# Merging the entry of the attention into its tile loop, with the exponentials made head by head on ScalarE

## The reference

```
x = x + graph_network(layernorm(x))                  # ends in batch norm and relu
h = layernorm(x)
weights = softmax(((h @ W_x + b_x) @ W_slice + b_slice) / temp)   # over the 64 slices of a head
norm    = weights.sum(over the nodes)
token   = einsum("bhnc,bhng->bhgc", h @ W_fx + b_fx, weights) / (norm + 1e-5)
...                                                  # attention among the 64 tokens of a head
x = x + (weights applied to the tokens) @ W_out + b_out
x = x + hypergraph_network(layernorm(x)); x = x + experts(layernorm(x))
```

## Time and profile before

| what | value |
|---|---|
| time, median of 3 runs | 2929.48 us (2929.36 to 2931.73) |
| the profiled execution, its time | 2930.67 us |
| its span in the profile | 2928.9 us |
| TensorE busy | 2408.9 us (82%) |
| VectorE busy | 1091.7 us (37%) |
| ScalarE busy | 388.4 us (13%) |
| GpSimd busy | 879.8 us (30%) |
| entry of the attention | about 1548 to 1575 us of the span |
| attention loop | about 1575 to 1710 us |

### The profile page before, as it was taken

How to read it: one execution, slowest core, us unless ns; L and a number is a source line. 1 busy time by engine, 2 the same in 40 slices (tenths; PEclk the granted TensorE clock), 3 DMA queues, 4 the chain that set the end, 5 groups by cost and what they waited for, 6 DMA issues and landing times.

```text
span 2928.9 us, 40346 instructions
## 1 busy us (share of the span) xinstructions
PE 2408.9 (82%) x14486; PEld 1801.0 (61%) x14486; DVE 1091.7 (37%) x2853; ACT 388.4 (13%) x839; POOL 879.8 (30%) x627
## 2 busy tenths in 40 slices
PE   5285556832759999999996879999999995999997
PEld 2151113521547776777773347888888884888886
DVE  7688885502321011111116855112220577111111
ACT  0030000000015000005002212000110002222221
POOL 6888887788830000000002410000000000233332
PEclk6595557976979999999997979999999997999999
DMA  9922226926460999990351000444344434567766
GB/s 340 293 1 0 0 1 216 287 2 168 75 179 0 233 249 266 186 204 0 101 191 51 0 0 1 129 146 131 123 140 151 149 126 136 169 202 213 209 188 176
DMA packets 297780, 397.71 MB, mean 136 GB/s; under 512 B 177973, under 2 KB 241228, under 8 KB 297610
## 3 DMA queue, kind: packets, MB, share of 16 engines
q1 hardware_dynamic: 115530, 268.24, 28.9%
q10 hardware_dynamic: 109760, 108.20, 14.0%
q0 software_dynamic: 72400, 20.04, 8.2%
HBM read 279.30 MB, written 99.82 MB: 129 GB/s over the span
## 4 chain that ended last, share of the span: by engine, by line
PE 60%; POOL 15%; DVE 8%; issue 7%; DMA 6%; ACT 1%; ACTq 1%; DVEq 1%; POOLq 0%; SPq 0%
PE ps L1919 14%; PE ps L2218 8%; PE ps L2219 8%; POOL at_counts L595 7%; POOL odd_counts L595 7%; PE ps L2312 7%; PE ps L2303 7%; PE ps L1846 4%; DMA odd_counts<-tarena 3%; PE ps L1937 3%; PE ps L2050 2%; PE ps L2151 2%; PE ps L2174 2%; DMA at_counts<-harena 2%; DVE late L1127 1%
## 5 line engine op out<-in xcount | busy, mean ns | idle before, releaser
L2218 PE MATMUL ps<-harena,ring 128*128 128x257 f16 (+1 forms) x2500 | 551.5, 272 | 8.0 <-DVE harena L1513 3.6
L2219 PE MATMUL ps<-harena,ring 128*128 128x256 f16 x2500 | 551.3, 271 | 0.0
L1919 PE MATMUL ps<-ring,harena 128*128 128x320 f16 x3800 | 511.8, 297 | 1.4 <-ACT tarena L758 0.8
L1919 PEld LDWEIGHTS ps<-ring,harena 128*128 128x128 f16 x3800 | 371.6, 98 | 138.1 <-issue 3.1
L595 POOL DMA_INDIRECT at_counts<-harena x208 | 332.5, 1599 | 89.7 <-issue 79.0
L595 POOL DMA_INDIRECT odd_counts<-harena x208 | 328.1, 1578 | 72.4 <-issue 60.9
L1127 DVE SCALAR_TENSOR_TENSOR late<-ps,ring 128x512 f16<-128x512 f32 x416 | 287.3, 746 | 21.5 <-issue 18.4
L1808 PE MATMUL ps<-harena,ident 104*128 104x512 f32 x208 | 187.4, 1018 | 117.7 <-DVE late L1127 116.7
L2218 PEld LDWEIGHTS ps<-harena,ring 128*128 128x128 f16 x2500 | 243.2, 97 | 44.2 <-DVE harena L1551 5.6
L2219 PEld LDWEIGHTS ps<-harena,ring 128*128 128x128 f16 x2500 | 241.7, 97 | 31.1
L1937 PE MATMUL ps<-feat,wl 128*128 128x320 f32 x448 | 126.2, 443 | 112.9 <-DVE feat L1209 111.8
(11 more groups left out here) (394 smaller groups left out, 2444.9 us busy)
## 6 DMA issues: line engine op xcount, KB each, us to landing
ring<-at_counts SPq DMA_DIRECT2D x145, 800.0 KB
ring<-L_ffn_W SPq DMA_DIRECT2D x64, 1024.0 KB, 5.1
ring<-ad_counts SPq DMA_DIRECT2D x50, 800.0 KB
at_counts<-tarena ACTq DMA_DIRECT2D x5, 4000.0 KB
odd_counts<-tarena ACTq DMA_DIRECT2D x5, 4000.0 KB
at_counts<-ring ACTq DMA_DIRECT2D x25, 800.0 KB
ad_counts<-xrows ACTq DMA_DIRECT2D x25, 800.0 KB, 8.0
xrows<-odd_counts SPq DMA_DIRECT2D x20, 800.0 KB
```

The source lines that it names most:

```text
L1919: ins = M(ps[:, 2 * f + h, 0:c], part[:, t, (2 * k + f) * P:(2 * k + f + 1) * P], chunk[q][:, s, h * HB:h * HB + c], start=(t == 0 and par ...
L2218: M(ps[:, i, 0:wide], lhs, hh[:, t, 0:wide], start=(t == 0), stop=False)
L2219: ins = M(ps[:, i, 0:F], lhs, hl[:, t, :], start=False, stop=(t == T - 1))
```

## The change

The entry is no stage of its own any more.

- ScalarE rectifies in place, `tfeat` to `tfeat`, all five blocks in one go.
- TensorE turns the first ENTRY_AHEAD = 7 tiles in front of the loop (`entry_turn`), into banks 0 to 3, and tile t+7 in the turn of tile t, into bank 6. The bias of the logits is spread before that, into bank 7.
- VectorE adds seven tiles and takes their statistics ahead of the loop, and the others in it, one a turn, at the turn's end. The variances, the root and the reciprocal are now made block by block (`entry_variance`, `entry_sqrt`, `entry_scale`, at the places that `stats_block` names: behind turns 2, 7, 12 and 17 for blocks 1 to 4).
- The loop is written out in full on all four engines, and the order in a turn is another: VectorE normalizes tile t+1, then does the shift of tile t-1, then the softmax of tile t-2; TensorE makes the tokens of tile t-3.
- VectorE no longer subtracts the maximum and no longer sums the heads: it negates the 8 maxima. ScalarE makes the exponentials in eight activations of 64 columns, with the negated maximum as bias and the head's sum as accumulator output.

```diff
+        ENTRY_AHEAD = 7
+        def stats_block(t):
+            b, k = divmod(t + ENTRY_AHEAD + 1, BT)
+            return b - 1 if k == 0 and 1 <= b - 1 < NB else None
+        def entry_bank(t):
+            return t % 4 if t < ENTRY_AHEAD else 6
...
 ScalarE
-            with act.Fori(0, NB) as b:
-                wait(tps, b * BT + 1)
+            for b in range(NB):
                 for f in range(2):
-                    nc.scalar.activation(feat[:, f, :], tfeat[:, f, nodes(b)], ACT.Relu,
+                    nc.scalar.activation(tfeat[:, f, nodes(b)], tfeat[:, f, nodes(b)], ACT.Relu,
...
-            ln_sqrt(5)
+            def entry_sqrt(b):
+                wait(ln_var, 5 + b)
+                tiles = slice(b * BT, b * BT + BT)
+                nc.scalar.activation(ln_s[:, tiles], ln_r[:, tiles], ACT.Sqrt).then_inc(ln_std, 1)
+            entry_sqrt(0)
...
-            def f_exps(t, i):
+            def f_exps(t):
                 wait(f_sub, t + 2)
-                nc.scalar.activation(logit[:, i % 3, :], logit[:, i % 3, :], ACT.Exp).then_inc(f_exp, 1)
+                for h in range(HEADS):
+                    columns = logit[:, t % 3, h * G:(h + 1) * G]
+                    ins = nc.scalar.activation(columns, columns, ACT.Exp, bias=hmax[:, t % 3, h:h + 1],
+                                               accum_out=hsum[:, t % 3, h:h + 1])
+                ins.then_inc(f_exp, 1)
...
-            three_stages(act.Fori(1, NB), f_copy, f_exps, f_weights)
+            for t in range(T + 3):
+                if t < T:
+                    f_copy(t, t % BT)
+                if t >= 1 and stats_block(t - 1) is not None:
+                    entry_sqrt(stats_block(t - 1))
+                if 1 <= t <= T:
+                    f_exps(t - 1)
+                if t >= 3:
+                    f_weights(t - 3)
...
 VectorE
-            dve.wait_ge(ent[3][1], T + 1)
-            layernorm_stats(5)
+            def add_gnn(t):
+                dve.wait_ge(tps, t + 2)
+                V.tensor_tensor(xrows[:, t, :], ps[:, entry_bank(t), 0:F], xrows[:, t, :], ALU.add).then_inc(lo, 1)
+                dve.wait_ge(lo, t + 2)
+                o.mark(V.bn_stats(ln_st[:, t, :], xrows[:, t, :]))
+            def entry_variance(b):
+                o.settle()
+                norm_variance(slice(b * BT, b * BT + BT))
+            def entry_scale(b):
+                tiles = slice(b * BT, b * BT + BT)
+                dve.wait_ge(ln_std, 5 + b)
+                step(V.reciprocal(ln_r[:, tiles], ln_s[:, tiles]))
...
-                V.tensor_tensor(logit[:, s, :].rearrange(H8, h=HEADS), logit[:, s, :].rearrange(H8, h=HEADS),
-                                hmax[:, s, :].unsqueeze(2).to_broadcast([P, HEADS, G]), ALU.subtract).then_inc(f_sub, 1)
+                V.tensor_scalar(hmax[:, s, :], hmax[:, s, :], -1.0, None, ALU.mult).then_inc(f_sub, 1)
...
-                step(V.tensor_reduce(hsum[:, s, :], logit[:, s, :].rearrange(H8, h=HEADS), AX.X, ALU.add))
                 step(V.reciprocal(hrec[:, s, :], hsum[:, s, :]))
-                if not isinstance(t, int) or t >= 2:
-                    dve.wait_ge(f_sum, t)
-                dve.wait_ge(f_used, t + (BT - 1))
+                if t >= 3:
+                    dve.wait_ge(f_sum, t - 1)
+                    dve.wait_ge(f_used, t + BT - 2)
...
-            three_stages(o.loop_from(1, NB, 4 * BT), f_normal, f_shift, f_softmax, third_early=True)
+            for t in range(ENTRY_AHEAD):
+                add_gnn(t)
+                if t == BT - 1:
+                    entry_variance(0)
+            entry_scale(0)
+            f_normal(0, 0)
+            for t in range(T + 2):
+                if t + 1 < T:
+                    f_normal(t + 1, (t + 1) % BT)
+                if 1 <= t <= T:
+                    f_shift(t - 1)
+                if t >= 2:
+                    f_softmax(t - 2)
+                if t + ENTRY_AHEAD < T:
+                    add_gnn(t + ENTRY_AHEAD)
+                if stats_block(t) is not None:
+                    entry_variance(stats_block(t))
+                if t >= 1 and stats_block(t - 1) is not None:
+                    entry_scale(stats_block(t - 1))
...
 TensorE
+            pe.wait_ge(x_in, 48)
+            M(ps[:, 7, :], ones[0:1, :], slice_bias[:, :], start=True, stop=True).then_inc(f_lg, 1)
+            def entry_turn(t):
+                pe.wait_ge(rows, t // BT * 2 + 2)
+                if t >= ENTRY_AHEAD:
+                    pe.wait_ge(lo, t + 1)
+                elif t >= 4:
+                    pe.wait_ge(lo, t - 2)
+                for f in range(2):
+                    ins = nc.tensor.transpose(ps[:, entry_bank(t), f * P:(f + 1) * P], tfeat[:, f, t * P:(t + 1) * P], ident[:, :])
+                ins.then_inc(tps, 1)
+            for t in range(ENTRY_AHEAD):
+                entry_turn(t)
...
-            three_stages(pe.Fori(1, NB), f_turn, f_logits, f_tokens)
+            for t in range(T + 3):
+                if t < T:
+                    f_turn(t, t % BT)
+                if t + ENTRY_AHEAD < T:
+                    entry_turn(t + ENTRY_AHEAD)
+                if 1 <= t <= T:
+                    f_logits(t - 1, (t - 1) % BT)
+                if t >= 3:
+                    f_tokens(t - 3, (t - 3) % BT)
```

More of the change, by code:

```diff
@@ L645, in _ @@
             pool.wait_ge(late_w, 16 * 17)
-            with pool.Fori(0, NB) as b:
-                for i in range(BT):
-                    r = bass.ds(b * BT + i, 1)
-                    pool.wait_ge(f_rows, b * BT + (i + 1))
-                    pool.nop(nofuse=True)
-                    nc.gpsimd.tensor_tensor(xrows[:, r, :], xrows[:, r, :], bout.unsqueeze(1), ALU.add).then_inc(f_bias, 1)
-                    pool.wait_ge(f_sw, b * BT + (i + 1))
-                    pool.wait_ge(f_sum, b * BT + (i + 1))
-                    pool.nop(nofuse=True)
-                    nc.gpsimd.tensor_tensor(weight_sum, weight_sum, sweight[:, i % 3, :], ALU.add).then_inc(f_sum, 1)
+            for t in range(T):
+                pool.wait_ge(f_rows, t + 1)
+                nc.gpsimd.tensor_tensor(xrows[:, t, :], xrows[:, t, :], bout, ALU.add).then_inc(f_bias, 1)
+                pool.wait_ge(f_sw, t + 1)
+                pool.wait_ge(f_sum, t + 1)
+                nc.gpsimd.tensor_tensor(weight_sum, weight_sum, sweight[:, t % 3, :], ALU.add).then_inc(f_sum, 1)
             pool.wait_ge(c_x, NB)
@@ L885, in block_sqrt @@
             def block_sqrt(b):
-                wait(ln_var, 6 + b)
+                wait(ln_var, 5 + NB + b)
                 tiles = slice(b * BT, b * BT + BT)
@@ L939, in route_sqrt @@
                 blk = bass.ds(b * BT, BT)
-                wait(ln_var, b * 2 + (NB + 6 + k))
+                wait(ln_var, b * 2 + (2 * NB + 5 + k))
                 nc.scalar.activation(ln_s[:, blk], ln_r[:, blk], ACT.Sqrt).then_inc(ln_std, 1)
@@ L2062, in _ @@
             pe.wait_ge(agg[2][0], NB * 2 + 2)
-            with pe.Fori(0, NB) as b:
-                pe.wait_ge(rows, b * 2 + 2)
-                for i in range(BT):
-                    pe.wait_ge(lo, b * BT + (2 if i == 4 else 1))
-                    for f in range(2):
-                        ins = nc.tensor.transpose(ps[:, i % 4, f * P:(f + 1) * P], feat[:, f, i * P:(i + 1) * P], ident[:, :])
-                    ins.then_inc(tps, 1)
+            pe.wait_ge(x_in, 48)
[11 more added lines that the diff above has]
+                entry_turn(t)
             pe.sem_inc(f_used, BT)
@@ L2088, in f_logits @@
                 pe.wait_ge(f_tcp, t + 2)
-                pe.wait_ge(f_sub, t + (2 - before(i)))
+                pe.wait_ge(f_sub, max(t, 1))
                 for d in range(2):
-                    ins = M(ps[:, i % 2, :], feat[:, d, i * P:(i + 1) * P], wxs[:, d, :], start=(d == 0), stop=(d == 1))
+                    ins = M(ps[:, t % 2, :], feat[:, d, i * P:(i + 1) * P], wxs[:, d, :], start=(d == 0), stop=(d == 1))
                 ins.then_inc(f_lg, 1)
```

41 lines of the change are left out of this document (14 added, 27 removed).

## The result

The changed kernel takes 2912.22 us (median of 4 runs, 2910.68 to 2918.32) against 2929.42 before: ratio 0.9933, 95% interval 0.9903 to 0.9962. Five more runs gave 2915.05 (2910.21 to 2919.93), ratio 0.9952 (0.994 to 0.9965). It is faster by 0.5 to 0.7%, and the forecast of 2914.4 lies between the two medians. The sum behind the forecast was less good than that, as the two traces show when only the changed stage is measured.

What follows compares the result with a forecast made beforehand. It took a relay entry with little overlap, then a loop with VectorE and TensorE near their end, as the bound. Entry -17.5, fill +0.5, loop +0.9, drain +1.0 made -15.1 us: 2914.4 us, range 2903 to 2922.

Steps and rivals of the forecast that it cites:

- Entry, -17.5 us: Ahead of the loop: in-place rectification and only seven tiles up front bring the first normalization 17.5 us earlier.
- The knot, 5.22 us: Loop with entering tiles: bank 6 waits for VectorE's addition, logits queue behind its transposes, next shift waits; 5.22 us a turn.
- 16 of them: Loop: the number of turns with tiles still entering, each put at 5.22 us; 8 turns without entering tiles follow.
- Stats turns, +1.5: Four loop turns with a block's variance: seven tiny VectorE instructions beside GpSimd cost 0.3 to 0.5 us each, 1.5 in all.
- Cold start, +2.9: First loop turns: TensorE at the half clock for one and a half turns, each 1.9 us dearer, +2.9 us.
- Turns without entering tiles, 4.35: Last 8 loop turns: TensorE's own work sets 4.35 us a turn, the middle of 4.2 and 4.47.
- Drain, +1.0: Behind the last shift: longer uncovered exponentials and one more token step, less subtraction and sums, +1.0 us.
- Exponentials, 2.7 us a tile: ScalarE in the loop: eight 64-column activations with accumulator take 2.7 us a tile (2.0 to 3.6), hidden except at the drain.
- The first (the knot does not bind): Loop rival, chance 0.12: all turns take 4.35 us, 13.9 us less, 2900.5 us in whole.
- The second (clock): Loop rival, chance 0.07: TensorE's clock stays low; all 16 turns at half clock give +36 us, near 2965.
- The third: Stats turns rival, chance 0.12: a table switch holds ScalarE twice its load, 2.6 us more each; +5.6 us, 2920.0.
- The fourth rival: Loop rival, chance 0.05: ScalarE becomes the bound, deciding from 0.53 us a head; at 0.6 the kernel takes 2943 us.

Runs made afterwards that it cites:

- a_swap: The changed kernel with TensorE issuing a tile's logits ahead of the entry transposes of tile t+7; 2894.86 us, ratio 0.9892 to the kernel before.
- a_early: The changed kernel with VectorE's addition and statistics of tile t+7 moved ahead of the softmax of tile t-2; 2899.82 us, ratio 0.9902 to the kernel before.
- a_wide: The changed kernel with the old softmax: one 512-column exponential, subtraction and head sums on VectorE; 2938.19 us, ratio 1.0039 to the kernel before.
- a_busy: The changed kernel with eight unneeded one-column ScalarE operations behind each tile's exponentials; 2911.22 us, ratio 0.9927 to the kernel before.
- a_noroot: The changed kernel with a copy in place of the block variances' square root, so no table switches in the loop; 2908.18 us, ratio 0.992 to before.
- b_heads: The kernel before with only the exponentials head by head, without VectorE's subtraction and head sums; 2944.72 us, ratio 1.0049 to the kernel before.

## Why the prediction was right, and where its sum was off

The direction, the place of the gain and the thing that paces the loop came out as written. By its steps:

- **Entry, -17.5 us**: -17.8.
- **Fill, +0.5**: 6.30 against 5.83, +0.5.
- **The knot, 5.22 us**: 5.16 in most turns, with both waits predicted (0.65 for "0.6", 1.15 for "about 1.3"). a_swap and a_early each open it, a_wide lengthens it by what it adds.
- **"16 of them"** is right for the knot, but 8 turns without entering tiles was one too many. From shift 16 to 17 VectorE still adds tile 24 and does its block's statistics, without a transposed tile behind it on TensorE, and that took 5.48 us: 17 turns with VectorE's addition and 7 without, +0.9. The 17 were 0.7 cheaper in all than 5.22 and 4.32 for the first.
- **Stats turns, +1.5**: 0.3 each, 1.2. They are what VectorE's work takes beyond the knot, not a part of the knot.
- **Cold start, +2.9: off by 1.6.** One turn ran at a mean clock of 0.75 and cost 1.3; in two other runs of kernels with the same start the clock was 1.00 and it cost nothing. I had taken one and a half turns at the half clock.
- **Turns without entering tiles, 4.35**: 4.08 on the mean, -1.9 over seven, the largest miss in the loop. Even the lower of my two bounds, 4.2 by starts, was too high.
- Together the loop was 118.2 us, not 121.8: -2.8 in place of +0.9.
- **Drain, +1.0**: from tile 24's shift to its tokens it is 5.48 us against 4.59, the +0.9 that I meant. But the stage's end came 0.4 earlier, not 1.0 later, since the last token matmuls and transposes ran faster: the granted clock from their start to the stage's end was 1.00, and 0.64 before. After (timeline):

```profile
1694.68 0.20 DVE L1423 RECIPROCAL harena<-harena 128x8 f32<-128x8 f32 x1 [1.94 <-ACT harena L882]
...
1695.72 1.98 PE L2143 MATMUL ps<-harena,feat 128*128 128x512 f32 x4 [0.50 <-DVE harena L1427]
1697.55 0.60 PE L2145 MATMUL ps<-ident,harena 128*128 128x128 f32 x4
```

  Before, the last two of these rows:

```profile
1706.68 2.83 PE L2098 MATMUL ps<-harena,feat 128*128 128x512 f32 x4 [2.03 <-DVE harena L1405]
1709.31 1.06 PE L2101 MATMUL ps<-ident,harena 128*128 128x128 f32 x4
```

  TensorE stood idle for 2.03 us ahead of them before and for 0.50 in after. VectorE waits for the exponentials here and nowhere else in the loop, as said.
- **Exponentials, 2.7 us a tile**: 2.65, ScalarE is at 39.03 of 50 us. Not on the path while tiles enter: a_busy. Behind the last table loads they are, through the copy that stands behind them: TensorE waits 1.19 us for it from shift 18 to 19.

So -20.5 in the terms of the sum (-17.8, +0.5, -2.8, -0.4) against -15.1, and -20.8 counted to the first matmul on the heads. By that the median of 2929.42 would have become 2908.6. It became 2912.22 and 2915.05, so the executions of after must have lost 3.6 and 6.3 us elsewhere. In the two profiled ones it was ahead of the stage; for the others that is inferred. That the recorded time was met is luck, and not part of the argument.

**The rivals.** The first (the knot does not bind) is refuted by the rows and by a_swap. The second (clock) happened in one turn of the 24. The third needed a switch to hold ScalarE for 2.6 us. ScalarE in after, end of the third block:

```profile
1660.98 0.36 ACT L876 ACTIVATE feat<-ps 128x256 f32<-128x256 f32 x1
1661.37 1.28 ACT L865 ACT_TABLE_LOAD   x1
1662.66 0.21 ACT L865 ACTIVATE ln_s<-ln_r 128x5 f32<-128x5 f32 x1
1662.89 1.28 ACT L882 ACT_TABLE_LOAD   x1
1664.18 0.35 ACT L882 ACTIVATE harena<-harena 128x64 f32<-128x64 f32 x1
```

Nothing is ahead of a load (0.03 us) nor behind it (0.01): a switch costs 1.29 us. The one turn where the loads were felt, from shift 18 to 19, cost 0.8 us (a_noroot), not 5.6 in all. The Trainium skill ("ScalarE: Activation LUTs", What ACT_TABLE_LOAD costs) adds a drain of some 1380 ns; these rows don't show it, and the measurement decides. The fourth rival wanted 0.53 us a head; it was 0.33.

**The two parts need each other.** Exponentials by head alone: +13.2 us in the stage (b_heads). The merged entry alone: +5.6 (a_wide). Together: -20.5. The merge turns VectorE's order round (shift first), which gives the exponentials a whole turn (VectorE waits for them only at the drain), and the exponentials take 1.25 us off the circle that the merge ties.

**Where the rest of the gain was.** VectorE's softmax lost 1.25 us a turn, and in 17 of the 24 turns it took over an addition and statistics. The loop got 2.8 us shorter in 24 turns, because the single bank tied the addition's end to the next logits. Two calls exchanged give 14.3 us more. a_swap, 2894.86 us, ratio 0.9892 to before, is the fastest of the complete kernels run. A second bank for the entering tiles was not tried.

## What to carry to other kernels

Before adding up the engines' work for a turn, walk the waits once round: a buffer that one engine frees at the end of its turn and another fills ahead of something urgent makes a circle whose length is a sum over both, while neither engine is full. Put the instruction that waits for a late release behind the urgent one. Here it took 14.3 us off the loop, where the whole rework had taken 2.8. And test the parts of a change apart: two that each lose by themselves can win together, and a kernel's total can hit a forecast whose terms are off.

## What the runs showed of the hardware

- ScalarE's accumulator is read by an instruction of its own, 0.19 us in the record, but the next activation starts 0.09 to 0.10 after its start. An exponential of 64 columns with it has a pitch (from start to start) of 0.333 us. The five of 128x56 without it in the earlier trace rows have 0.236: 1.27 less the 0.33 of one, over four. By an estimate from the two, it costs some 0.09 a head.
- VectorE's small operations grow beside GpSimd's. In a block's statistics 128x5 operations that take 0.15 to 0.17 us took 0.54 and 0.70 (1607.11 and 1607.65 in after). Each ended within 0.03 us of the end of an operation of GpSimd. A normalization took 1.36 in place of 0.41:

```profile
1664.25 1.27 POOL L658 TENSOR_TENSOR late<-late,harena 128x512 f32<-128x512 f32 x1 [3.51 <-DVE harena L1427]
1664.31 1.36 DVE L1087 TENSOR_SCALAR feat<-xrows,ln_mv,ln_r 128x256 f32<-128x256 f32 x1
```

  It ended 0.15 us behind GpSimd's end. The Trainium skill ("SBUF — State Buffer", SBUF: two separate sides) says that the two share a pair of ports, which whoever starts first keeps for its whole instruction; for VectorE this holds of operations in a two-port mode, or with two inputs in SBUF beside a GpSimd operation that reads SBUF. The times agree with that rule; which of the two cases the normalization is, no row shows.
- The turn from shift 1 to 2 ran at a granted clock of 0.75 and 0.74 in the two profiled executions of after (6.77 and 6.64 us) and of 1.00 in a_busy and a_noroot (5.48 and 5.47). TensorE's and VectorE's programs are the same in all four; ScalarE's differ. So 1.3 us of such a turn can come from the clock alone.
- Later turns can have a lower clock too. In a_wide two of them, both behind a block's statistics, ran at 0.83 and 0.90 and took 7.61 and 7.03 us, where its usual turn at 1.00 took 6.41.
